# A shifted-window transformer block: first norm by per-column statistics on VectorE, projection bias added by GpSimd

## What is computed

```
h = roll(layernorm(x) * g1 + b1, (-4, -4))        # over the 64 channels, eps 1e-5
q, k, v = windows8x8(h) @ qkv_w + qkv_b           # 16 windows of 64 pixels an image, 4 heads of 16
attn = softmax(q k^T / 4 + rpb + shift_mask)
x = x + roll(unwindow((attn v) @ proj_w + proj_b), (4, 4))
h2 = layernorm(x) * g2 + b2
out = x + gelu_tanh(h2 @ fc1_w + fc1_b) @ fc2_w + fc2_b      # 64 -> 256 -> 64
```

## Time and profile before

| | |
|---|---|
| runs | 516.42 us median of 3 (514.03, 516.42, 518.35) |
| profiled execution: span from first to last instruction | 516.1 us |
| PE busy | 462.7 us, 90% |
| DVE busy | 388.9 us, 75%, 549 instructions |
| ACT busy | 359.0 us, 70% |
| POOL busy | 384.4 us, 74% |

### The profile page before, as it was taken

One profiled execution on the slowest core, in us unless ns is written; L12 is line 12 of the kernel. 1 busy time (PEld: TensorE's weight loads), 2 busy tenths in 40 slices (PEclk: granted clock), 3 DMA queues, 4 the chain that ended last, 5 costly groups with the idle time before them and its releaser, 6 DMA issues.

```text
span 516.1 us, 21507 instructions
## 1 busy us (share of the span) xinstructions
PE 462.7 (90%) x9630; PEld 352.7 (68%) x9630; DVE 388.9 (75%) x549; ACT 359.0 (70%) x501; POOL 384.4 (74%) x376
## 2 busy tenths in 40 slices
PE   0765799999899999999999999998799999999995
PEld 0533587787788788778788778677566666666664
DVE  2865688899779899879899899894467767666752
ACT  0236488878878878778778778775577777777761
POOL 2648959879969979969969978942288888888830
PEclk9998799999999999999999999999999999999999
DMA  8201424411411411411011011000003303311333
GB/s 162 60 1 31 99 47 96 114 34 25 104 38 30 104 39 28 102 34 37 23 29 40 23 25 41 24 23 3 3 3 84 84 12 74 84 46 40 83 83 83
DMA packets 9986, 27.04 MB, mean 52 GB/s; under 512 B 3368, under 2 KB 3368, under 8 KB 7976
## 3 DMA queue, kind: packets, MB, share of 16 engines
q1 hardware_dynamic: 9896, 25.68, 21.1%
HBM read 9.15 MB, written 8.39 MB: 34 GB/s over the span
## 4 chain that ended last, share of the span: by engine, by line
PE 53%; DVE 17%; POOL 16%; ACT 8%; issue 2%; DMA 2%; SPq 0%; ACTq 0%; DVEq 0%
PE work L693 20%; PE outs L693 10%; POOL probs L367 9%; PE trans L693 8%; PE scores L693 6%; DVE negmax L482 5%; DVE probs L476 4%; POOL stat_rstd L333 4%; PE scores L829 3%; PE trans L789 3%; DVE x L517 3%; DMA params<-in_params 2%; POOL xn L344 2%; DVE x L533 2%; ACT qT L605 2%
## 5 line engine op out<-in xcount | busy, mean ns | idle before, releaser
L367 POOL TENSOR_TENSOR probs<-probs,negmax 128x1024 f32<-128x1024 f32 x64 | 123.9, 1937 | 38.4 <-DVE negmax L482 38.4
L333 POOL TENSOR_TENSOR stat_rstd<-stat_var,minus_half 128x8 f32<-128x8 f32 (+1 forms) x62 | 105.0, 1693 | 5.0
L476 DVE TENSOR_TENSOR probs<-scores,bias 128x1024 f32<-128x1024 f32 x64 | 77.9, 1218 | 32.9 <-PE scores L693 32.9
L638 ACT ACTIVATE probs<-probs 128x1024 f32<-128x1024 f32 x64 | 67.7, 1058 | 50.3 <-POOL probs L367 49.8
L338 POOL TENSOR_TENSOR xn<-x,stat_mean 128x256 f32<-128x256 f32 (+1 forms) x91 | 77.2, 867 | 4.1
L482 DVE TENSOR_REDUCE negmax<-probs 128x16 f32<-128x1024 f32 x64 | 78.1, 1220 | 2.2
L693 PEld LDWEIGHTS work<-params,probs 128*64 128x64 f32 x2048 | 62.2, 138 | 23.5 <-DVE x L570 20.5
L693 PE MATMUL scores<-kX,qT 32*64 32x128 f32 x2048 | 71.5, 276 | 7.2 <-DVE probs L476 4.6
L693 PE MATMUL outs<-vX,probsT 128*64 128x34 f32 x2048 | 72.9, 226 | 5.1 <-ACT probsT L643 4.1
L693 PEld LDWEIGHTS outs<-vX,probsT 128*64 128x64 f32 x2048 | 66.0, 139 | 16.4 <-issue 9.5
L789 PEld LDWEIGHTS trans<-ident,probs 128*128 128x128 f32 x512 | 56.2, 142 | 26.4 <-issue 14.2
(11 more groups left out here) (64 smaller groups left out, 691.7 us busy)
## 6 DMA issues: line engine op xcount, KB each, us to landing
kX<-kT SPq DMA_DIRECT2D x124, 64.0 KB, 2.0
x<-in_x SPq DMA_DIRECT2D x32, 224.0 KB
out<-x SPq DMA_DIRECT2D x28, 224.0 KB
x<-in_x SPq DMA_DIRECT2D x32, 32.0 KB
out<-x SPq DMA_DIRECT2D x28, 32.0 KB
out<-x SPq DMA_DIRECT2D x16, 56.0 KB
params<-in_params SPq DMA_DIRECT2D x1, 741.5 KB, 12.3
out<-x SPq DMA_DIRECT2D x16, 8.0 KB
```

Source lines behind the costliest of these rows:

```text
L333: nc.gpsimd.tensor_tensor(stat_rstd[:, cols], stat_var[:, cols], minus_half[:, cols], ALU.pow).then_inc(ln_rstd, pieces)
L367: nc.gpsimd.tensor_tensor(e, e, top, ALU.add).then_inc(shifted, 1)
L476: nc.vector.tensor_tensor(e[:, :].rearrange("q (u a m) -> q a u m", u=2, a=2), scores[:, :].rearrange("q (a u m) -> q a u m", a=2, u=2), b ...
L638: nc.scalar.activation(probs[n % 4][:, :], probs[n % 4][:, :], ACT.Exp)\
```

## The change

1. **First norm.** VectorE takes `bn_stats` of each image column (64 channels; 32 instructions a group), which gives mean and sum of squared deviations of the even and of the odd channels. From these, once a group, come the negated mean, the variance and, by three Newton steps from an integer guess, the root: `first_roots` (9 instructions) and `last_roots` (7), on 32 columns each, nearly all dependent on the one before through a semaphore. GpSimd adds the mean and multiplies (`normal`), in whole pieces of `xn` (two passes of 512 columns; the last piece four of 256). Its pow and small ops and ScalarE's squares go.
2. **Places.** Relative to the group's first step: statistics at -7 to -4, `first_roots` at -2 (step 6 of the group before), `last_roots` at 0, `normal` at 0 to 3. Group 1: statistics at -1, -1, 0, 0, roots at 0 and 1, `normal` at 1, 1, 2, 3.
3. **Projection bias.** `add_y_bias` goes from VectorE (steps 3 and 5) to GpSimd (steps 4 and 6), at the end of GpSimd's `norm(n)`.
4. **Start.** SP waits for load(0) before it issues load(1), and issues load(2) right behind. Group 0 is normed by 16 `tensor_scalar` of VectorE (64 columns each), 8 `activation` of ScalarE and one `normal` of GpSimd. VectorE scales `wqkv` only behind its 16.

```diff
-LN_STEPS = {"sum": (-4, -4, -3, -2), "mean": (-4, None, -3, -2), "centre": (-4, -4, -3, -2),
-            "square": (-2, -1, 0, 1), "square_sum": (-1, 0, 1, 2), "rstd": (-1, 0, 1, 2),
-            "scale": (0, 1, 2, 3)}
...
+LN1_STEPS = {"stats": (-7, -6, -5, -4), "first_roots": (-2,), "last_roots": (0,), "normal": (0, 1, 2, 3)}
+
+LN1_STEPS_FIRST = {"stats": (-1, -1, 0, 0), "first_roots": (0,), "last_roots": (1,),
+                   "normal": (1, 1, 2, 3)}
...
             load(0)
             sp.dma_start(params[:, :], params_d).then_inc(params_in, 16)
+            sp.wait_ge(x_loaded[0], 16 * COPIES)
             load(1)
+            load(2)
...
+            def normal(g, j):
+
+                for dst, src, m in zip(of_xn(j), of_x(g, j), of_stat(neg_mean, j)):
+                    done = nc.gpsimd.tensor_tensor(dst, src, m, ALU.add)
+                done.then_inc(x_centred, 1)
+                pool.wait_ge(x_centred, PIECES * (g - 1) + j + 2 if g else 1)
+                for dst, r in zip(of_xn(j), of_stat(ln_scale, j)):
+                    done = nc.gpsimd.tensor_tensor(dst, dst, r, ALU.mult)
+                return done
...
             def norm(n):
...
+                for group, j in ln1_at("normal", n):
+                    pool.wait_ge(ln1_made, group + 1)
+                    if j in (0, 2):
+
+                        pool.wait_ge(work_ready["XT"], COUNT["XT", group - 1, j // 2])
+                    normal(group, j).then_inc(xn_ready, 1)
...
+                if n >= 0 and n % STEPS in (4, 6):
+                    add_y_bias(n // STEPS, (n % STEPS - 4) // 2)
...
+            def row_stats(g, i):
+
+                for c in range(i * WIN, (i + 1) * WIN):
+                    done = nc.vector.bn_stats(ln_stats[:, c, :], x[:, g * ROW + c * C:][:, 0:C])
+                done.then_inc(stats_made, 1)
+
+            def first_roots(g):
...
+                nc.vector.tensor_tensor(ln_between[:, :], *means, ALU.subtract).then_inc(root_steps, 1)
+                nc.vector.scalar_tensor_tensor(ln_within[:, :], within[0], C * EPS, within[1],
+                                               ALU.add, ALU.add).then_inc(root_steps, 1)
+                nc.vector.tensor_tensor(ln_twice_mean[:, :], *means, ALU.add).then_inc(root_steps, 1)
+                dve.wait_ge(root_steps, before + 1)
+                nc.vector.tensor_tensor(ln_between[:, :], ln_between[:, :], ln_between[:, :], ALU.mult)\
+                  .then_inc(root_steps, 1)
...
+            def last_roots(g):
+
+                before = ROOT_STEPS * g
+                dve.wait_ge(root_steps, before + 9)
+                nc.vector.scalar_tensor_tensor(ln_root[:, :], ln_step[:, :], 1.5, ln_root[:, :],
+                                               ALU.add, ALU.mult).then_inc(root_steps, 1)
+                dve.wait_ge(root_steps, before + 10)
+                nc.vector.tensor_tensor(ln_step[:, :], ln_root[:, :], ln_root[:, :], ALU.mult)\
+                  .then_inc(root_steps, 1)
...
             dve.wait_ge(x_loaded[0], 16 * COPIES)
             for i in range(PIECES):
-                row_sum(x[:, i * PIECE:(i + 1) * PIECE], i)
...
+                row_stats(0, i)
+            first_roots(0)
+            last_roots(0)
+            dve.wait_ge(ln1_made, 1)
+            nc.vector.tensor_tensor(first_shift[:, :], neg_mean[:, :], ln_scale[:, :], ALU.mult)\
+              .then_inc(first_shift_made, 1)
+            for j in range(2):
+                for c in range(SHIFT):
+                    for w in range(2):
+                        at = column_of(j, c, w)
+                        done = nc.vector.tensor_scalar(
+                            xn_v[:, 0, SHIFT * j + c, w, :], x[:, at * C:(at + 1) * C],
+                            neg_mean[:, at:at + 1], ln_scale[:, at:at + 1], ALU.add, ALU.mult)
+                done.then_inc(xn_first[0], 1)
...
                     if kind == "Y":
                         add_y(of, i)
                 norm(n)
-                if n < PAIRS and n % STEPS in (3, 5):
-                    add_y_bias(n // STEPS, (n % STEPS - 3) // 2)
```

More of the change, by code:

```diff
@@ L98, in tasks_at, with ln1_at, ln2_at @@
     return [task[1:] for task in TASKS if task[0] == n]
-LN_STEPS = {"sum": (-4, -4, -3, -2), "mean": (-4, None, -3, -2), "centre": (-4, -4, -3, -2),
-            "square": (-2, -1, 0, 1), "square_sum": (-1, 0, 1, 2), "rstd": (-1, 0, 1, 2),
-            "scale": (0, 1, 2, 3)}
[L106 to L111, removed]
+LN1_STEPS = {"stats": (-7, -6, -5, -4), "first_roots": (-2,), "last_roots": (0,), "normal": (0, 1, 2, 3)}
+LN1_STEPS_FIRST = {"stats": (-1, -1, 0, 0), "first_roots": (0,), "last_roots": (1,),
+                   "normal": (1, 1, 2, 3)}
+def ln1_at(stage, n):
     found = []
[L115 to L118, removed]
-    return found
+    for group in range(1, GROUPS):
+        steps = LN1_STEPS_FIRST if group == 1 else LN1_STEPS
+        found += [(group, i) for i, at in enumerate(steps[stage]) if STEPS * (group - 1) + at == n]
+    return found
+LN2_STEPS = {"sum": (-4, -4, -3, -2), "centre": (-4, -4, -3, -2),
+             "square": (-2, -1, 0, 1), "square_sum": (-1, 0, 1, 2), "rstd": (-1, 0, 1, 2),
+             "scale": (0, 1, 2, 3)}
+def ln2_at(stage, n):
+    return [i for i, at in enumerate(LN2_STEPS[stage]) if STEPS * (GROUPS - 1) + at == n]
 PARAM_COLUMNS = [("wqkv", 3 * P), ("gain", 2), ("shift", 2), ("bqkv", 3), ("turn", 2), ("bf1", 2), ("bproj", C),
@@ L392, in _, with add_y_bias @@
-            norm(-1)
+            def add_y_bias(g, half):
+                if g:
+                    pool.wait_ge(x_centred, PIECES * g + 1)
+                else:
+                    pool.wait_ge(y_bias_made, 1)
+                    pool.wait_ge(xn_first[0], 2)
+                    pool.wait_ge(xn_first[1], 1)
+                    pool.wait_ge(x_centred, 1)
+                dst = x[:, g * ROW + half * 2 * PIECE:][:, 0:2 * PIECE].rearrange("q (a f) -> q a f", f=C)
+                nc.gpsimd.tensor_tensor(dst, dst, y_bias[:, :].unsqueeze(1).to_broadcast([P, 2 * WIN, C]),
+                                        ALU.add).then_inc(y_biased, 1)
@@ L615, in take @@
                     done.then_inc(v_copied, 1)
-            for j in range(PIECES):
-                square(j, j, PIECES)
+            act.wait_ge(first_shift_made, 1)
+            for c in range(SHIFT):
+                for w in range(2):
+                    at = column_of(2, c, w)
+                    done = nc.scalar.activation(
+                        xn_v[:, 1, c, w, :], x[:, at * C:(at + 1) * C], ACT.Identity,
+                        bias=first_shift[:, at:at + 1], scale=ln_scale[:, at:at + 1])
+            done.then_inc(xn_first[1], 1)
             act.wait_ge(biases_summed, 1)
@@ L687, in _ @@
                 if PIECES <= s + 3 < S:
-                    square(S + s + 3, (s + 3) % PIECES, S + s + 4)
+                    square(s + 3)
         @block.tensor
```

265 lines of the change are left out of this document (146 added, 119 removed).

## The result

The changed kernel takes 536.04 us (median of 4 runs, 535.31 to 539.2), the kernel before, run beside it, 516.51 (4 runs, 514.03 to 518.35). The ratio is 1.040, interval 1.035 to 1.044: 19.5 us lost where I had forecast 11.5. The profiled execution took 535.33 us, its span is 533.5.

The account below looks back on a forecast made before the run. TensorE was taken to bound the kernel, busy 188.0 of 196.8 us in the even groups. 516.1 - 6.6 (loop gain) + 18.0 (root stops) + 2.6 (start) - 2.4 (first group) - 0.1 (end) = 527.6, so 528 us; range 508 to 536.

Parts of the forecast that it names:

- The mechanism: Steps 6 and 0: VectorE's short root operations wait for GpSimd's long instructions, delaying TensorE; +18.0 us in all, chance 0.58.
- The chain of turns at step 6: first_roots wait for GpSimd's shift, then for its bias addition; TensorE stands 1.45 us each time.
- the single turn at step 0: last_roots wait for GpSimd's shift, so bias_and_max and the division come late; TensorE stands 1.4 us.
- the gain: Groups 1 to 6: TensorE's irregular stops at the V projection go, -1.1 us a group, -6.6 us in all.
- Rival A: Loop: short root operations don't meet GpSimd, or slip in, so only the gain remains; 508 us, chance 0.17.
- B: Rival: shift is waited for, but first_roots keep the bias addition out; step 6 free, step 0 stays; 518.5 us, chance 0.15.
- Links: Root chains: each dependent operation of 32 columns takes 0.21 us, bounds 0.15 to 0.28.
- the lower bound of the loop's sum: Stops at steps 6 and 0 over six groups: 11 us if each dependent root operation takes 0.15 us, against +18.0 forecast.
- The start: Up to the first score: VectorE's norm of group 0 delays the wqkv scalings; first score +2.6 us, bounds 0 to 5.5.
- its queue of shift(n+1) behind them is not late by my hand schedule: Loop: GpSimd has room for its added work, so the next shift comes in time; no loss counted.
- rival C: The forecast plus half speed for 14 us more after TensorE's idle start and a late first group: +7, 535 us, chance 0.10.
- The first group: After the first score: pows, squares and scalings around the first shifts go; -2.4 us, bounds -4.2 and +1.

Follow-up runs that it names:

- experiment 3: The changed kernel with GpSimd's two bias additions at steps 5 and 7 in place of 4 and 6: 521.75 us, ratio 1.009.
- before_load_alone: The kernel before with only the change's order of loads (load 0 waited for, then loads 1 and 2): 513.62 us, ratio 0.998.
- between_5_7: The changed kernel, root chains between bias addition and maximum, GpSimd's bias additions at steps 5 and 7: 520.56 us; a second version with wqkv scaled ahead of the tensor_scalars: 517.7.

## Why the prediction was wrong

**The mechanism and its size held.** The chain of turns at step 6 and the single turn at step 0 are in the trace as I had laid them on the earlier trace rows, down to GpSimd's addition taking the second turn. A stretch was to grow by 2.85 us where the gain alone would leave it; undisturbed it is 41.45 against 38.5, +2.95. By place I had 1.45 and 1.4: the stops are 1.69 and 1.27, while the prices by experiment 3 are 2.1 and 0.8. So the sum is nearer than its terms, and that is partly luck. The gain was 0.8 us a group (39.3 to 38.5), not 1.1: a stop of V that goes leaves other waits behind. Rival A is out (its text also counts 1.9 us less in the first group, which its sum, 508, does not use). B's mechanism is not what happens, but experiment 3 makes its case, a free step 6, and gives 521.75.

The Trainium skill, "SBUF — State Buffer", section "Who interferes with whom", calls the port pair that VectorE shares with GpSimd an exclusive lock. The trace agrees here for the shift and the bias addition: 0.2 us operations waited for the end of whole GpSimd instructions of 1.90 and 2.37 us.

**The terms.** bn_stats stand 0.13 us apart (4.16 for 32), for my 0.14. Links are 0.22, for 0.21; with the 13 links a group at 0.15 us the lower bound of the loop's sum would have been about 13, not 11. GpSimd's bias addition takes 2.37 us, for my 1.9, which I took from the shift: this is most of why step 6 cost more. The start gave +1.6 for +2.6: VectorE ran as forecast (the first warming starts at 24.65, forecast 24.5), but from there to the first score it is 11.7 us (24.65 to 36.31) where it was 12.9 (21.90 to 34.75): the products come to their full speed earlier in the chain, the first transposes of `xn` taking 1.04 us, where they took 1.84.

**The step that failed** is "its queue of shift(n+1) behind them is not late by my hand schedule". It held for the six groups over which I drew it. At step 52 the second norm has two passes ahead of the bias addition, and I had looked at the last group's end only at n = 61 to 63. The shift waited there for three instructions, and TensorE stood 2.55 us. It made the seventh stretch +4.0 us, where my terms gave +0.3 (the gain, and the roots of step 48).

**The clock.** The second term that was missing is the half clock, for which the sum had nothing in the loop or in the MLP, which I carried over unchanged. Before, TensorE had 10.2 us of it between the first score and the last microseconds; after, 23.8 us. All four that begin later than 60 us follow stops of TensorE. The first is at the first meeting, where there is no Y fill and the stop is 1.9 us:

```profile
77.53 1.10 PE L797 MATMUL scores<-kX,qT 32*64 32x128 f32 x32 [1.91 <-DVE probs L581]
79.41 1.93 PE L797 MATMUL outs<-vX,probsT 128*64 128x34 f32 x32 [0.78 <-DVE o_rows L596]
```

One follows the stop at step 52, another the change to the MLP (+1.6 us there), one adds 1.2 us to the third stretch. The 13.6 us more cost at most half, 6.8. That the stops bring the half clock is not shown: the stops of 0.9 and 0.78 us ahead of 164.0 come in five groups alike and are followed by it in one, and ahead of the MLP both kernels stand the same 0.57, 1.34 and 1.68 us, before (L693) at the full clock and after (L797) at half:

```profile
366.73 1.13 PE L693 MATMUL trans<-xT,w 64*128 64x512 f32 x4 [1.68 <-DVE x L533]
...
382.54 2.08 PE L797 MATMUL trans<-xT,w 64*128 64x512 f32 x4 [1.68 <-DVE x L635]
```

The other kernels have these stops too: in eight 3.4 to 10.2 us of half clock lie there, in before_load_alone and the two between_5_7 none. The sum comes out as rival C's (14 us at half speed, 535), but not for its reason: I had tied it to the idle start, whose products ran faster than before (3.35 us for 3.78 in the first warming), and had given it 0.10. The first group did gain at its head (the outs product at 58.67, 1.3 us sooner after the first score, and at 1.13 us for the 1.93 of the earlier trace rows), and lost it at 79.41. Together, with my terms laid on the stretches as -0.05 for the first and +1.75 for each of the next five: stretch 7 missed by 3.7, the MLP by 1.6, the first six by 2.1, the start by -1.0, the tail by -0.5. That is 5.9 of the 8 us. The other 2.1 lie between the profiled executions and the medians.

**Open:** what decides where the half clock falls, why the bias addition is slower on GpSimd than the shift of as many columns (2.37 against 1.90 us), what TensorE would lose to a chain at the old place that nothing holds, and why between_5_7's second stretch is 39.98 and not 39.35.

## What to carry to other kernels

Look for the place of a short VectorE operation with two SBUF inputs by what GpSimd is doing at that moment: two chains of mostly dependent 0.2 us operations a group cost 19 us beside GpSimd's long ones and nothing where GpSimd was waiting for VectorE anyway. Moving such work off a meeting brought back nearly all that it had cost; shortening it was not tried. Each move has to be checked for the next meeting that it makes. Draw the schedule for the irregular groups too (first, last), for such a stop comes on top of the regular ones, and the half clock that followed it here (3.4 us) cost up to another 1.7.

## What the runs showed that I had not expected

- The two chains, sixteen operations a group, between the bias addition and the maximum, directly ahead of the shift, cost nothing: 517.38 us with them and 517.39 without them.
- GpSimd's tensor_tensor of 1024 columns took 1.90 us with a maximum repeated over 64 columns each, and 2.37 us with 64 columns repeated 16 times.
- Stops of 1.91 and 2.55 us, with TensorE at the full clock before them, were followed by 6.8 and 3.4 us at 1.2 GHz; the same stops of 0.57, 1.34 and 1.68 us ahead of the MLP were followed by 3.4 us of it in the changed kernel and by none in the kernel before.
- Holding back the second load brought the first score 1.8 us forward on the kernel before.
